# Four new tables for the order of work on the engines of a six-stage graph-network kernel

## The chip, the cores and the metric

The kernel runs on one core of a Trainium2 chip. The metric is the time on the device in microseconds (us), the median of several runs. Five engines work side by side: TensorE (PE in the profile, matmuls into PSUM banks), ScalarE (ACT), VectorE (DVE), GpSimd (POOL), and SyncE (SP), which here only issues DMAs. Each takes its own instructions strictly in the order in which they were written and stops at one that waits for a semaphore.

## The reference

128 graphs of 64 nodes with 256 features pass four graph layers; after each comes `x = layernorm(x + layer(x))`. Cut to what is computed, with `adj` the weighted adjacency matrix of a graph:

```python
def layer0(x):                       # hypergraph convolution, twice
    H = (adj != 0); B = 1 / H.sum(axis=1); Dn = 1 / (H @ adj[first row])
    conv = lambda x, W, b: Dn * (H @ (B * (H.T @ (x @ W.T)))) + b
    h = layernorm(relu(conv(x, W1, b1))) * gamma + beta
    return conv(h, W2, b2) + x
def layer1(x):
    q, k = split(x @ Wqk); v = x @ Wv
    w = mask * sum(q * (adj @ (k * mask)), -1) / 16
    return softmax(w, over nodes) * v
def layer2(x):                       # 8 heads of 32
    s = (q @ k.T) * 32 ** -0.5 * (adj + adj)
    return (softmax(s) @ v) @ Wo.T + bo
def layer3(x):
    xg = x * sigmoid(adj.sum(-1) * Wd + bd)
    QK = sigmoid(xg @ Wqk.T + bqk)
    s = (QK @ QK.T) / 16 * adj
    out = (s / (s.sum(-1) + 1e-6)) @ xg
    return relu(out @ Wl.T + bl + xg @ Wr.T)
```

## The kernel before

Four graphs (256 node rows, two tiles of 128) make a group; there are 32 groups. Every float32 product is made of two float16 parts: a value is cast to float16 on ScalarE (names ending in `h`), the remainder is formed on VectorE or GpSimd (names ending in `l`), and a product is three matmuls, L460 to L462. A block of 12 such matmuls with 256 columns is TensorE's common unit.

The work of a group is cut into six streams (0 to 5), each a Python generator on each engine that gives up control at every `yield`. In a step `s`, stream `k` works on group `s - k`, so six groups are under way at once and 32 groups take 37 steps. The first six and the last steps have fewer streams; a hardware loop over two steps holds the middle. Stream 0 is the first convolution of layer 0, stream 1 the second one and the first half of layer 1, stream 2 the softmax of layer 1 and the query of layer 2, stream 3 keys, values, scores and the exponentials, stream 4 the context, the output projection and the gate of layer 3, stream 5 the rest of layer 3.

What sets the order within a step is one list per engine, `ORDER_PE`, `ORDER_ACT`, `ORDER_DVE` and `ORDER_POOL`: each entry is the number of the stream that may do its next piece (the code up to its next `yield`). SyncE's order is written out apart and does not depend on the lists. All waits are on semaphores that are counted upwards, so any order that does not deadlock computes the same.

Pieces of TensorE that the text names: `m&d` (L519 to L525, HBh and wch into bank A), `pT` (L530, the turn of `Pf`), `z1`, `z01` and `z23` (the two halves of the projection with W1, together 24 matmuls), `rsum` (L556 to L560, sums of `rF` and of `rsq` over the features), `y0` (the product of `rF` and W2, in two halves `y0a` and `y0b`), `conv2` (y0 with P), `x1T` and `x2T` and `xgT` and `cxT` (L485, four transposes each), `u` and `ux`, `wT` (L595), `prT` (L598), `v1`, `q`, `k`, `v`, the two score blocks (L634), `eT0` and `eT1` (L645), the two context blocks (L658), `Wo`, `qk3`, `y3`, `s3`, `o2` (its L460 reads Wr), and the attention's row sums (L702).
On GpSimd: `gp` (L1217, bias of the gate), `xres` (L1217), `y0l`, `xl`, `rFl` (L1200), `Ssb0` and `Ssb1` (L1287, late<-late,Smx, the two shifts of the scores), the two sums of `rsq` (L1242, L1245), `xg` (L1299, late<-g,late), `am` (L1269), and for each layer norm K the small `veK`, `rsK`, `nbK`.
On VectorE: `preG` (L1176) and `rFl` of the second half (L999), both of two SBUF inputs; `o3` (L1171), the masked scores `Sm0`, `Sm1` (L1102), `rvar` (L1008), `wpr` (L1066), `Ql` (L1148), `HBl`, `x1Fl`, `x2Fl`, `ul`, `xgFl`, `PTl` and others of L894.
The tiles `late` hold several of these values.

SyncE copies the keys into a block-diagonal tile `Kbd` with four DMAs (L374) once their low half `kst` is there (L370), and the values likewise into `Vbd` (L384); between the two it issues the loads of the next step.

Of the kernel before, what the change touches and what calls it, by code (L numbers as in the profile page):

```python
# [40 lines left out]
QK3 = 0.25 / 16.0  # L41
HUGE = 3e38

ORDER_PE = [4, 2, 5, 4, 1, 3, 0, 5, 4, 3, 2, 0, 1, 5, 0, 2, 4, 0, 0, 5, 3, 1, 5, 3, 5, 2, 1, 3, 2, 1, 0, 3, 4, 0]
ORDER_ACT = [5, 0, 4, 2, 5, 1, 3, 5, 0, 4, 0, 3, 4, 0, 5, 4, 1, 0, 0, 0, 5, 2, 1, 0, 0, 0, 2, 3, 1, 4, 3, 2, 4, 3, 5]
ORDER_DVE = [0, 4, 0, 4, 0, 4, 0, 2, 0, 2, 4, 0, 1, 4, 2, 0, 0, 0, 2, 2, 5, 3, 5, 2, 4, 0, 1, 5, 1, 1, 0, 2, 2, 4, 2, 4, 4, 3, 3, 5, 3, 3, 1, 3, 5, 2, 5, 1, 0, 5, 5, 5, 3, 1, 1, 0, 4, 2, 0, 3, 0]
ORDER_POOL = [0, 0, 0, 1, 4, 1, 0, 3, 1, 1, 5, 1, 2, 2, 4, 2, 4, 0, 5, 3, 4, 0, 3, 0, 4, 1, 5, 5, 5, 0, 0, 0]

LAST_LAG = 5
STEPS = GROUPS + LAST_LAG  # L50
# [3 lines left out]
def build(nc, x, adj, adj_t, mask, mask_col, w1t, b1, gamma, beta, w2t, b2, wqk1t, wv1, wqt, bq, wkt, bk, wvt, bv,  # L54
          wot, bo, wqk3t, bqk, wlt, bl, wrt, wd, bd, out):
    ctx = ExitStack()
    with ctx:
# [213 lines left out]
        def run(eng, order, streams):  # L271


            def step(j, s, lo, hi):
                live = {k: streams[k](At(k, j, s)) for k in range(lo, hi + 1)}
                for k in order:
                    if k in live:
                        next(live[k], None)
                assert all(next(live[k], "end") == "end" for k in live)

            first = LAST_LAG + 1
            last = first + (GROUPS - first) // 2 * 2
            for s in range(first):
                step(None, s, 0, s)
            with eng.Fori(first // 2, last // 2) as j:
                for par in range(2):
                    step(j, par, 0, LAST_LAG)
            for s in range(last, STEPS):
                step(None, s, max(0, s - GROUPS + 1), LAST_LAG)
# [167 lines left out]
        def _(pe):  # L457
# [254 lines left out]

            run(pe, ORDER_PE, [stream0, stream1, stream2, stream3, stream4, stream5])


        @block.scalar
        def _(act):
# [168 lines left out]

            run(act, ORDER_ACT, [stream0, stream1, stream2, stream3, stream4, stream5])


        @block.vector  # L890
        def _(dve):
# [291 lines left out]

            run(dve, ORDER_DVE, [stream0, stream1, stream2, stream3, stream4, stream5])


        @block.gpsimd
        def _(pool):
# [123 lines left out]

            run(pool, ORDER_POOL, [stream0, stream1, stream2, stream3, stream4, stream5])

# [38 lines left out]
```

How the kernel before makes its waits and increments, by code:

```python
            def load_conv(at):  # L326
                if at.earlier(2):
                    sp.wait_ge(ev("x_lo"), at.n(-2)).then_inc(ev("sp_held"), 1)
                sp.dma_start(xin[:, at.par], at_group(xv, at)).then_inc(ev(f"x_in{at.par}"), 16)
                if at.earlier(2):
                    sp.wait_ge(ev("h_t"), at.n(-2)).then_inc(ev("sp_held"), 1)
                    sp.wait_ge(ev("w_lo"), at.chain(3, 3, -2)).then_inc(ev("sp_held"), 1)
                blocks(atA, adj_t, at, "at_in")
# [1 line left out]
            def load_residual(at):  # L335
                if at.earlier(2):
                    sp.wait_ge(ev("preB"), at.n(-2)).then_inc(ev("sp_held"), 1)
                sp.dma_start(xres[:, at.par], at_group(xv, at)).then_inc(ev(f"xres_in{at.par}"), 16)
# [1 line left out]
            def load_layer1(at):  # L340
                if at.earlier(2):
                    sp.wait_ge(ev("adj_masked"), at.n(-2)).then_inc(ev("sp_held"), 1)
                    sp.wait_ge(ev("w_masked"), at.n(-2)).then_inc(ev("sp_held"), 1)
                blocks(aC, adj, at, "C_in")
                sp.dma_start(mrow[:, at.par], mr[bass.ds(at.group(), 1)].rearrange("g o k -> (g o) k")
                             .broadcast_to([P, TOK])).then_inc(ev(f"C_in{at.par}"), 16)
                sp.dma_start(mcol[:, at.par], mask_col[bass.ds(at.group(), 1)].rearrange("g p t -> (g p) t")
                             ).then_inc(ev(f"C_in{at.par}"), 16)
# [107 lines left out]
        @block.tensor  # L456
# [31 lines left out]
            pe.wait_ge(ev("w2_scaled"), 1)
            for k in range(4):
```

## Time and profile before

| what | before |
|---|---|
| median of 3 runs | 1060.98 us (1060.03 to 1066.08) |
| profiled execution, span | 1059.4 us (nothing outside its span is recorded) |
| TensorE busy | 956.5 us, 90% |
| VectorE busy | 886.8 us, 84% |
| GpSimd busy | 777.8 us, 73% |
| ScalarE busy | 710.6 us, 67% |
| instructions | 32426 |

Busy time is a share of the span; fill and drain of the pipeline count in it. An idle engine is listed with what ended its idle time. The chain of waits is followed back from the last instruction; where it shows "issue", the engine waited for nothing that the profile records.

### The profile page before, as it was taken

To read this page: it belongs to the slowest core of one execution; us is meant where nothing else is said; L and a number is where in the kernel's file an instruction comes from. 1 tells how busy PE (TensorE), PEld (TensorE's weight loads), DVE (VectorE), ACT (ScalarE), POOL (GpSimd) and SP (SyncE) were. 2 spreads that over 40 slices of the span, in tenths; PEclk is the share of its full clock that TensorE was granted. 3 is DMA by queue.
4 is the path that set the end of the run, shared out by engine and by line. 5 is a ranking of instruction groups with operands and counts; after the bars stand their busy time and mean duration, and the time that the engine had idled before them with its cause. 6 is when DMAs were issued, how large, how long until landed. Compare 5 with 4: busy or idle time off the path is not lost.

```text
span 1059.4 us, 32426 instructions
## 1 busy us (share of the span) xinstructions
PE 956.5 (90%) x11164; PEld 808.6 (76%) x11164; DVE 886.8 (84%) x2564; ACT 710.6 (67%) x1516; POOL 777.8 (73%) x1163
## 2 busy tenths in 40 slices
PE   3368999999999999999999999999999999999873
PEld 2256788888888888888888888888888888887752
DVE  4346888898989989989998998989999998989862
ACT  2335677777776677777776677777776777776642
POOL 3155778778877788788877788788877887786542
PEclk9589999999999999999999999999999999999986
DMA  7110221222222122222222112222212112211110
GB/s 206 31 33 9 64 61 53 69 68 59 67 57 61 51 53 57 67 57 67 67 55 62 50 52 60 67 57 67 67 53 62 50 51 62 67 45 42 46 39 20
DMA packets 110231, 61.80 MB, mean 58 GB/s; under 512 B 57072, under 2 KB 105840, under 8 KB 110192
## 3 DMA queue, kind: packets, MB, share of 16 engines
q1 hardware_dynamic: 110192, 61.30, 22.2%
q8 instruction: 22, 0.36, 0.2%
q14 instruction: 17, 0.14, 0.0%
HBM read 35.83 MB, written 8.39 MB: 42 GB/s over the span
## 4 chain that ended last, share of the span: by engine, by line
DVE 33%; PE 25%; issue 14%; ACT 13%; POOL 12%; DMA 1%; DVEq 1%; SPq 0%; POOLq 0%; ACTq 0%
PE bank L460 7%; PE bank L462 6%; PE bank L461 6%; DVE preG L1176 4%; DVE rFl L999 3%; ACT x L735 3%; POOL y0l L1200 3%; ACT r L762 2%; DVE late L1171 2%; PE bank L485 2%; DVE ql L900 2%; PE bank L634 2%; DVE stG L947 2%; DVE PTl L894 2%; DVE xgFl L894 2%
## 5 line engine op out<-in xcount | busy, mean ns | idle before, releaser
L1102 DVE TENSOR_TENSOR late<-bank,acD 128x512 f32<-128x512 f32 x64 | 44.2, 690 | 51.3 <-PE bank L634 50.9
L735 ACT ACTIVATE x<-preB,nbB,rsB 128x256 f32<-128x256 f32 x64 | 35.0, 593 | 68.0 <-POOL nbB L1212 68.0
L460 PE MATMUL bank<-z1h,W 128*128 128x256 f16 x256 | 71.0, 277 | 3.1 <-DVE z1l L894 3.0
L461 PE MATMUL bank<-z1l,W 128*128 128x256 f16 x256 | 70.9, 277 | 0.0
L460 PE MATMUL bank<-W,rFh 128*128 128x256 f16 x256 | 70.8, 277 | 0.0
L462 PE MATMUL bank<-z1h,W 128*128 128x256 f16 x256 | 70.8, 277 | 0.0
L462 PE MATMUL bank<-W,rFl 128*128 128x256 f16 x256 | 70.5, 275 | 0.0
L461 PE MATMUL bank<-W,rFh 128*128 128x256 f16 x256 | 70.5, 275 | 0.0
L1287 POOL TENSOR_TENSOR late<-late,Smx 128x512 f32<-128x512 f32 x64 | 67.0, 1046 | 0.0
L735 ACT ACTIVATE late<-preG,nbG,rsG 128x256 f32<-128x256 f32 x64 | 34.9, 593 | 47.0 <-POOL nbG L1212 46.9
L1200 POOL TENSOR_TENSOR y0l<-y,y0h 128x512 f16<-128x512 f32 x32 | 55.5, 1736 | 1.5 <-ACT y0h L719 1.5
L1299 POOL TENSOR_TENSOR late<-g,late 128x512 f32<-128x512 f32 x32 | 53.5, 1672 | 2.9 <-ACT late L735 2.9
L762 ACT ACTIVATE r<-bank,b1c 128x256 f32<-128x256 f32 x128 | 49.8, 462 | 5.7 <-PE bank L462 5.7
L1248 POOL TENSOR_SCALAR rve<-rvar 128x2 f32<-128x2 f32 x32 | 7.2, 224 | 61.7 <-DVE rvar L1008 61.7
L1176 DVE SCALAR_TENSOR_TENSOR preG<-late 128x512 f32<-128x512 f32 x32 | 51.3, 1604 | 0.1
L1200 POOL TENSOR_TENSOR rFl<-r,rFh 128x512 f16<-128x512 f32 x32 | 37.2, 1163 | 19.1 <-ACT rFh L719 18.7
L1217 POOL TENSOR_TENSOR gp<-late,bdb 128x512 f32<-128x512 f32 x32 | 40.7, 1272 | 11.1 <-ACT late L842 11.1
L719 ACT ACTIVATE xgFh<-bank 128x512 f16<-128x512 f32 x32 | 19.1, 597 | 44.2 <-PE bank L485 44.2
L634 PE MATMUL bank<-Kbd,qh 128*64 128x256 f16 x512 | 47.1, 279 | 1.2 <-DVE vst L894 1.2
L485 PE MATMUL bank<-ident,x 128*128 128x128 f32 x256 | 42.2, 288 | 5.9 <-ACT x L735 2.7
L460 PE MATMUL bank<-xgFh,Wqk 128*128 128x256 f16 x128 | 36.2, 283 | 12.3 <-DVE xgFl L894 12.3
L645 PE MATMUL bank<-ident,E 128*128 128x128 f32 x256 | 40.3, 281 | 4.9 <-ACT E L831 4.9
(284 smaller groups left out, 4625.1 us busy)
## 6 DMA issues: line engine op xcount, KB each, us to landing
Vbd<-vst SPq DMA_DIRECT2D x128, 66.0 KB, 2.1
xin<-x SPq DMA_DIRECT2D x32, 256.0 KB, 2.7
xres<-x SPq DMA_DIRECT2D x32, 256.0 KB, 2.8
Kbd<-kst SPq DMA_DIRECT2D x128, 64.0 KB, 2.0
out<-late SPq DMA_DIRECT2D x32, 256.0 KB, 2.2
mrow<-mask SPq DMA_DIRECT2D x32, 128.0 KB, 3.1
atA<-adj_t SPq DMA_DIRECT2D x64, 32.0 KB, 2.3
aC<-adj SPq DMA_DIRECT2D x64, 32.0 KB, 2.1
```

Of the source, the lines that this page charges most:

```text
L460: pe.matmul(o, sh, mh, start=start, stop=False, skip_group_check=True)
L461: pe.matmul(o, sh, ml, start=False, stop=False, skip_group_check=True)
L462: return pe.matmul(o, sl, mh, start=False, stop=stop, skip_group_check=True)
L485: m = pe.transpose(o[:, c * TOK + t * P:c * TOK + (t + 1) * P], src[:, t, c * P:(c + 1) * P], ident_[:])
L634: m = pe.matmul(o[64 * b:64 * b + 64, c * 256:(c + 1) * 256], qq[:, c, tok], Kbd[:, :, hl, c, tok], start=(i == 0), stop=(i == 2), skip_gr ...
L735: m = act.activation(dst[:, t], pre[k][:, t], ACT.Identity, bias=nb[k][:, t:t + 1], scale=rs[k][:, t:t + 1])
L762: m = act.activation(r[:, 2 * i + c], (bA, bB)[i][:, c * TOK:(c + 1) * TOK], ACT.Relu, bias=b1c[:, 2 * i + c:2 * i + c + 1], scale=1.0 / WS)
L1102: dve.tensor_tensor(Sm[:, t], (bD0, bD1)[t][:].rearrange("p (h k) -> p h k", h=HEADS), acD[:, at.par, t:t + 1].broadcast_to([P, HEADS, NOD ...
L1176: dve.scalar_tensor_tensor(out=pre["G"][:].rearrange("p t k -> p (t k)"), in0=o3[:].rearrange("p t k -> p (t k)"), scalar=0.0, in1=x3[:, a ...
L1200: return pool.tensor_tensor(dst, a, b, ALU.subtract)
L1287: pool.tensor_tensor(Ssb[:, t], Sm[:, t], Smx[:, t:t + 1].rearrange("p t h -> p h t").broadcast_to([P, HEADS, NODES]), ALU.subtract).then_ ...
L1299: pool.tensor_tensor(xg[:], g2[:], x3[:, at.par], ALU.mult).then_inc(ev("xg"), 1)
```

## The change

Only the four lists change. Each keeps its length and how often each stream stands in it; every piece is still done once a step. What moves is where a piece stands among those of other streams.

```diff
-ORDER_POOL = [0, 0, 0, 1, 4, 1, 0, 3, 1, 1, 5, 1, 2, 2, 4, 2, 4, 0, 5, 3, 4, 0, 3, 0, 4, 1, 5, 5, 5, 0, 0, 0]
+ORDER_POOL = [0, 0, 0, 1, 1, 0, 4, 3, 5, 1, 1, 1, 1, 2, 2, 2, 4, 5, 4, 3, 0, 4, 3, 0, 0, 4, 5, 5, 5, 0, 0, 0]
...
```

GpSimd, in the loop, from the statistics of layer 2's norm to the product `xg`; first before, then with the change. `late<-late,blb` is the bias of `o2`.

```order
L1208 TENSOR_TENSOR rsF<-veF,powm 128x2
L1200 TENSOR_TENSOR rFl<-r,rFh 128x512
L1217 TENSOR_TENSOR late<-late,blb 128x512
L1287 TENSOR_TENSOR late<-late,Smx 128x512
L1212 TENSOR_SCALAR nbF<-mvF,rsF 128x1 x2
L1242 TENSOR_TENSOR rsq<-rsq 128x512
L1287 TENSOR_TENSOR late<-late,Smx 128x512
L1245 TENSOR_TENSOR rsq<-rsq 128x256
L1299 TENSOR_TENSOR late<-g,late 128x512
```

The same place with the change:

```order
L1217 TENSOR_TENSOR late<-late,blb 128x512
L1208 TENSOR_TENSOR rsF<-veF,powm 128x2
L1287 TENSOR_TENSOR late<-late,Smx 128x512
L1200 TENSOR_TENSOR rFl<-r,rFh 128x512
L1212 TENSOR_SCALAR nbF<-mvF,rsF 128x1 x2
L1287 TENSOR_TENSOR late<-late,Smx 128x512
L1242 TENSOR_TENSOR rsq<-rsq 128x512
L1245 TENSOR_TENSOR rsq<-rsq 128x256
L1299 TENSOR_TENSOR late<-g,late 128x512
```

`rFl` has moved behind the first shift of the scores, and both sums of `rsq` behind the second. Further up the list `gp` moved from ahead of `y0l` to behind `xl`, `SAl` ahead of `veB`, and `am` from behind `xg` to behind `nbB`.

VectorE, in the loop, from the second masked score to the statistics of layer 3's norm; first before.

```order
L1102 TENSOR_TENSOR late<-bank,acD 128x512
L894 SCALAR_TENSOR_TENSOR x1Fl<-bank,x1Fh 128x512
L1107 TENSOR_REDUCE Smx<-late 128x8
L1165 RECIPROCAL srec<-ssum 128x2
L894 SCALAR_TENSOR_TENSOR x2Fl<-bank,x2Fh 128x512
L1171 SCALAR_TENSOR_TENSOR late<-bank,srec,late 128x256 x2
L894 SCALAR_TENSOR_TENSOR ul<-bank,uh 128x512
L999 TENSOR_TENSOR rFl<-r,rFh 128x512
L1176 SCALAR_TENSOR_TENSOR preG<-late 128x512
L947 BN_STATS stG<-preG 128x6 x2
```

The same place with the change:

```order
L1102 TENSOR_TENSOR late<-bank,acD 128x512
L1165 RECIPROCAL srec<-ssum 128x2
L1107 TENSOR_REDUCE Smx<-late 128x8
L894 SCALAR_TENSOR_TENSOR x1Fl<-bank,x1Fh 128x512
L1171 SCALAR_TENSOR_TENSOR late<-bank,srec,late 128x256 x2
L894 SCALAR_TENSOR_TENSOR x2Fl<-bank,x2Fh 128x512
L1176 SCALAR_TENSOR_TENSOR preG<-late 128x512
L894 SCALAR_TENSOR_TENSOR ul<-bank,uh 128x512
L999 TENSOR_TENSOR rFl<-r,rFh 128x512
L947 BN_STATS stG<-preG 128x6 x2
```

`o3` now stands ahead of `x2Fl`, `x1Fl` behind the second maximum, and `preG` ahead of `ul` and `rFl`. Elsewhere on VectorE `xgFl` moved from ahead of `ql` to behind `rvar`, `HBl` from ahead of `y0` to behind it, `Ql` from behind `wpr` to ahead of the three small divisions (L982 to L988), the low half of `k` (L900, kst) from behind `Ql` to behind `preB`, and `z1l` behind `preC`.

On TensorE the order of a step was ctx0, wT, qk3, ctx1, y0b, k, m&d, y3, cxT, v, prT, pT, conv2, s3, z1, v1, Wo, z01, z23, o2, scores 0, x1T, row sums, scores 1, o1, x2T, u, eT0, q, ux, rsum, eT1, xgT, y0a. It is now wT, ctx0, y0b, ctx1, qk3, k, y3, m&d, cxT, v, pT, conv2, prT, s3, z1, v1, Wo, o2, z01, scores 0, z23, row sums, scores 1, x1T, o1, x2T, u, q, eT0, ux, eT1, rsum, y0a, xgT. On ScalarE the main moves are `x1Fh` to ahead of the first `rFh` (it stood behind it), and the second `relu` behind the norm of layer 1.

## Rows read from the trace of the kernel before

**Rows 1.** The page: the span.

```profile
span 1059.4 us, 32426 instructions
```

**Rows 2.** Windows: us, then busy time (instructions) of PE, PEld, DVE, ACT, POOL, clock, DMA.

```profile
200.00:400.00 200.00, 193.64 (x2344) 165.94 (x2342) 183.16 (x538) 143.91 (x311) 160.47 (x239) 1.00 0.22 59
```

**Rows 3.** Timeline, VectorE, `rvar`: start us, us, what [idle before <- releaser].

```profile
147.01 0.15 DVE L1008 SCALAR_TENSOR_TENSOR rvar<-bank,rmm 128x2 f32<-128x2 f32 x1
...
953.98 0.14 DVE L1008 SCALAR_TENSOR_TENSOR rvar<-bank,rmm 128x2 f32<-128x2 f32 x1
```

**Rows 4.** Chain of waits, one step: start us, us in the chain, what.

```profile
503.94 0.60 DVE xgFl L894
...
510.25 0.10 POOL gp L1217
...
511.47 1.82 POOL y0l L1200
...
513.33 0.28 PE bank L460
...
527.02 0.87 DVE late L1171 x2
```

**Rows 5.** Timeline, GpSimd, the tail of its list.

```profile
522.26 1.16 POOL L1200 TENSOR_TENSOR rFl<-r,rFh 128x512 f16<-128x512 f32 x1
...
525.64 0.49 POOL L1212 TENSOR_SCALAR nbF<-mvF,rsF 128x1 f32<-128x1 f32 x2
526.10 1.27 POOL L1242 TENSOR_TENSOR rsq<-rsq 128x512 f32<-128x512 f32 x1
527.33 1.03 POOL L1287 TENSOR_TENSOR late<-late,Smx 128x512 f32<-128x512 f32 x1
528.34 0.72 POOL L1245 TENSOR_TENSOR rsq<-rsq 128x256 f32<-128x256 f32 x1
529.02 1.72 POOL L1299 TENSOR_TENSOR late<-g,late 128x512 f32<-128x512 f32 x1
```

**Rows 6.** Timeline, VectorE, first masked score and two `preG`.

```profile
522.98 0.69 DVE L1102 TENSOR_TENSOR late<-bank,acD 128x512 f32<-128x512 f32 x1 [1.85 <-PE bank L634]
...
529.53 1.75 DVE L1176 SCALAR_TENSOR_TENSOR preG<-late 128x512 f32<-128x512 f32 x1
...
1033.38 0.69 DVE L1176 SCALAR_TENSOR_TENSOR preG<-late 128x512 f32<-128x512 f32 x1
```

**Rows 7.** Timeline, TensorE, one step.

```profile
500.07 0.16 PE L556 MATMUL bank<-ones,rFh 128*128 128x1 f16 x1 [0.36 <-DVE rFl L999]
...
500.92 0.63 PE L645 MATMUL bank<-ident,E 128*128 128x128 f32 x4
501.39 0.60 PE L485 MATMUL bank<-ident,late 128*128 128x128 f32 x4
...
504.60 0.28 PE L460 MATMUL bank<-xgFh,Wqk 128*128 128x256 f16 x1 [0.34 <-DVE xgFl L894]
...
512.84 0.44 PE L530 MATMUL bank<-ident,Pf 128*128 128x128 f32 x2
...
517.99 0.27 PE L460 MATMUL bank<-z1h,W 128*128 128x256 f16 x1
...
520.61 0.27 PE L460 MATMUL bank<-Wr,xgFh 128*128 128x256 f16 x1
...
522.79 0.66 PE L485 MATMUL bank<-ident,x 128*128 128x128 f32 x4
```

**Rows 8.** Waits: waiting piece and who ended it: us in total, times, longest.

```profile
PEld bank L658 <- DVE PTl L894: 10.0, 42, 0.4
```

**Rows 9.** Timeline, ScalarE, the cast of `r`.

```profile
521.55 0.63 ACT L719 ACTIVATE rFh<-r 128x512 f16<-128x512 f32 x1
```

**Rows 10.** Timeline, SyncE's queue, the copies into `Kbd`.

```profile
513.27 2.48 SPq L374 DMA_DIRECT2D Kbd<-kst  x4
```

**Rows 11.** The page: DMA issues, KB each, median us to landing.

```profile
Kbd<-kst SPq DMA_DIRECT2D x128, 64.0 KB, 2.0
```

More of the change, by code:

```diff
@@ L42 @@
 HUGE = 3e38
-ORDER_PE = [4, 2, 5, 4, 1, 3, 0, 5, 4, 3, 2, 0, 1, 5, 0, 2, 4, 0, 0, 5, 3, 1, 5, 3, 5, 2, 1, 3, 2, 1, 0, 3, 4, 0]
-ORDER_ACT = [5, 0, 4, 2, 5, 1, 3, 5, 0, 4, 0, 3, 4, 0, 5, 4, 1, 0, 0, 0, 5, 2, 1, 0, 0, 0, 2, 3, 1, 4, 3, 2, 4, 3, 5]
-ORDER_DVE = [0, 4, 0, 4, 0, 4, 0, 2, 0, 2, 4, 0, 1, 4, 2, 0, 0, 0, 2, 2, 5, 3, 5, 2, 4, 0, 1, 5, 1, 1, 0, 2, 2, 4, 2, 4, 4, 3, 3, 5, 3, 3, 1, 3, 5, 2, 5, 1, 0, 5, 5, 5, 3, 1, 1, 0, 4, 2, 0, 3, 0]
-ORDER_POOL = [0, 0, 0, 1, 4, 1, 0, 3, 1, 1, 5, 1, 2, 2, 4, 2, 4, 0, 5, 3, 4, 0, 3, 0, 4, 1, 5, 5, 5, 0, 0, 0]
+ORDER_PE = [2, 4, 1, 4, 5, 3, 5, 0, 4, 3, 0, 1, 2, 5, 0, 2, 4, 5, 0, 3, 0, 5, 3, 1, 5, 2, 1, 2, 3, 1, 3, 0, 0, 4]
+ORDER_ACT = [0, 5, 2, 5, 1, 4, 5, 0, 3, 0, 4, 3, 4, 0, 5, 5, 1, 4, 0, 2, 0, 1, 0, 0, 2, 0, 0, 1, 3, 4, 3, 3, 2, 4, 5]
+ORDER_DVE = [4, 0, 4, 0, 2, 4, 0, 2, 0, 4, 0, 1, 0, 4, 5, 0, 2, 0, 2, 0, 2, 5, 0, 1, 2, 3, 4, 5, 1, 1, 2, 0, 2, 4, 2, 4, 3, 4, 3, 5, 3, 3, 5, 3, 1, 5, 2, 5, 1, 0, 5, 5, 1, 3, 0, 1, 3, 0, 2, 0, 4]
+ORDER_POOL = [0, 0, 0, 1, 1, 0, 4, 3, 5, 1, 1, 1, 1, 2, 2, 2, 4, 5, 4, 3, 0, 4, 3, 0, 0, 4, 5, 5, 5, 0, 0, 0]
 LAST_LAG = 5
```

## The prediction

> **What bounds the kernel now.** I read the busy line first, then the windows, the period, the chain of waits, and last the timelines of the engines where the chain passes. The span is 1059.4 us [rows 1]. The median of the shown runs is 1060.98, so 1.6 us lie around the profiled span; every sum below is a difference and is set on the median. In the filled pipeline TensorE is busy 193.64 of 200 us at full granted clock, VectorE 183.16, GpSimd 160.47 [rows 2]. So TensorE alone leaves some 3% to win, and only in the filled stretch. The reader should see that this stretch repeats: `rvar` starts at 147.01 and at 953.98 [rows 3], 27 intervals of 29.89 us. The other 252 us fill and drain the pipeline.
>
> The chain of waits shows why a step takes 29.89 us and not TensorE's 29. It runs through VectorE up to `rvar`, then down the GpSimd list (`gp` and `y0l` among it), enters TensorE at the second convolution at 513.33, stays there for twelve microseconds, and goes back to VectorE through `x2Fl`, `o3` (the tile `late` of L1171) and `rFl` [rows 4]. `xgFl`, `gp` and `o3` stand in it only because they are listed there; nothing in the chain reads their results.
>
> **What leaves the chain.** (1) `gp` moves behind `y0l` and `xl`. That frees 1.22 us, from 510.25 to 511.47 (the chain gives 0.10 to `gp` itself and the rest to no one, but GpSimd does nothing else in it) [rows 4]. `y0l` still needs `y0h`, which ScalarE can give no earlier than some 0.6 us after `y0`, so I count 1.0. (2) `xgFl` moves behind `rvar`: 0.60. (3) `o3` moves ahead of `x2Fl`, into a place where VectorE would otherwise stand by: up to 0.82. VectorE now idles 1.85 us before the first masked score [rows 6], and in the new TensorE list the first score comes one 1.31 us block earlier, so that idle shrinks. Counting these alone the step would be 29.89 - 1.0 - 0.6 - 0.8 = 27.5, below what TensorE can do. So this chain stops being the bound, and the question is which takes over.
>
> **TensorE's own work.** From the first row-sum matmul to the end of the first score block it takes 500.07 to 522.79, 22.72 us. Of this 0.34 is the wait for `xgFl` and 0.27 the wait for `y0l` (two transposes and the wait take 512.84 to 513.33, 0.49, where four take 0.47) [rows 7], and 10.0 us in 42 waits are for `PTl` [rows 8], some 0.3 a step. The new list puts `xgT` after `y0`, and both context blocks and `y0` ahead of `qk3`, so these three are covered: `xgFl` has 2.6 us of matmuls to hide in. Waits left out elsewhere (before `rsum` 0.36, before `x2T` 0.15 as an estimate) give about 28.1 to 28.4 for a step with no wait. That is the floor.
>
> **What takes over: the tail of the GpSimd list.** `rsum` on TensorE needs both sums of `rsq`. Before, `rFl` (its first half) stood ahead of the score shifts, and the longer sum ahead of the second shift. Now both are listed after: `Ssb0`, `rFl`, `nbF`, `Ssb1`, `rsq`, `rsq`. And on TensorE the turn of `x1` moves behind the second score block, on ScalarE `x1Fh` ahead of the first `rFh`. So `rFl` cannot start before all that. With 0 at the start of the second half of `z` (the block that now follows the first scores):
> - TensorE: 1.31 (half of the 2.62 from 517.99 to 520.61), row sums of the attention 0.15 (estimate: 4 matmuls of a kind of which 18 take 0.85), second scores 0.8 (520.61 to 522.79 holds one block of 1.31 and the first scores), `x1T` and its landing 0.6 [rows 7]: 2.86.
> - ScalarE: `x1Fh` 0.5, `rFh` 0.63 [rows 9]: 3.99.
> - GpSimd: `rFl` 1.16, `nbF` 0.46, `Ssb1` 1.01, `rsq` 1.23 and 0.68 [rows 5]: 8.53.
> - The lock between VectorE and GpSimd. Alone, `preG` takes 0.69; beside `xg` it takes 1.75, and `xg` takes 1.72 where the equally large `rsq` takes 1.27 [rows 5, 6]. Two instructions with two SBUF inputs do not run together: each delays GpSimd by about 0.45. Before, only `rFl` and `preG` met `xg`, after the last `rsq`. Now `preG` comes directly behind `x2Fl`, two instructions ahead of `rFl`, and by the sum both meet `Ssb1` and `rsq`, ahead of `rsum`: 0.9. That is 9.43.
> - To TensorE's start 0.36, as before `rsum` now [rows 7]: 9.79.
> - TensorE from `rsum` to the end of the first scores: 22.72 less `eT1` 0.47 (now ahead of `rsum`), less `z23` 1.31, less the covered waits 0.34 + 0.27 + 0.3 = 20.0.
>
> The sum is 29.8, with estimated terms that I rounded upwards by some 0.1; I take 29.7, 0.19 below 29.89. This is 27 x 0.19 = 5 us. With one lock instead of two it would be 27 x 0.6 = 16. In short, gains of 2.4 us in the old chain are nearly all taken by a new one.
>
> The Trainium skill (SBUF — State Buffer, section on two separate sides) says that VectorE and GpSimd share one port pair as an exclusive lock, held for a whole instruction, for VectorE operations with two SBUF inputs. The 0.69 against 1.75 agrees. By that rule `HBl`, too, which moves from ahead of `y0` to behind it, would stand behind `xres`; no row here shows `HBl` beside a long GpSimd instruction.
>
> **Smaller edits.** `am` moves from the tail to behind `nbB`, where GpSimd waits for VectorE's statistics; its cover is that wait, and if it is gone it delays `nbC` by at most 1.27 (what the larger `rsq` takes [rows 5]), some microseconds ahead of its use. `m&d` moves behind `y3`: the three small divisions on VectorE now wait for it, and `Pf` and `pT` stand behind them with only `cxT` and `v` (1.9 us) as cover, against about 2.1 of need. Between nothing and 1.2 us (if VectorE is late); I take 0 since `pT` is at TensorE's place with 0.2 to spare and keep the upper end for the range. `z1l` moves behind `preC`, with some 0.9 us to spare. Fill and drain keep their dependences; ten steps with some 0.4 us either way, 0 within 4.
>
> **Rivals.**
> (A) **TensorE alone sets the step.** If `preG` slips in ahead of `Ssb1`, or ScalarE's `rFh` comes sooner than I have it, the sums are ready when TensorE is. Against it: the sum of the GpSimd tail has no slack to lose. For it: 8.53 without locks gives 28.9, near TensorE's floor. Step 28.7: 1061 - 27 x 1.19 = 1029; range 1020 to 1045.
> (B) **The gain does not come at all:** `m&d` behind `y3` makes `pT` late by 0.3, on top of the forecast. Step 30.0: 1064; 1059 to 1070.
> (C) **Slower: the scores wait for `Kbd`.** The low half of `k` moves on VectorE behind `y3l`, `Pl`, `preB` and `pcol` (some 1.6 us), and the first scores come 1.31 us earlier. SyncE issues the four copies at 513.27 and needs 2.48 for them, the last lands 2.0 after its issue [rows 10, 11]: about 4.2 from the end of `kst` to data. Before, the scores began 4.8 us later than that. Now 4.8 - 1.6 - 1.3 = 1.9 are left, less 0.6 because TensorE is quicker between, less 0.7 because the small divisions wait. If the lock holds VectorE 1 us or more ahead of `kst` (`Ql` behind `y0l`, `wpr` behind `xl`), it decides: about 0.9 us a step more, 27 x 0.9 = 24, 1085; from 1072 to 1095. By the Trainium skill (SBUF — State Buffer, same section) `HBl` is one more that waits ahead of `kst`, which would make C likelier.
>
> **How the numbers follow.** A measurement of this kernel tells about 1% from no change; that is 1050.4 to 1071.6. Forecast 0.42: step 29.7, 1061 - 5 = 1056, its own range 1046 to 1061 with 0.08 of its chance below 1050. A 0.26, B 0.13, C 0.15, and 0.04 for something not seen, half to each side. Faster: 0.08 + 0.26 + 0.02 = 0.36. Within: 0.34 + 0.13 = 0.47. Slower: 0.15 + 0.02 = 0.17. The range reaches to the middle of A and leaves out most of C: 1026 to 1074.
>
> **What would show it.** `rvar` every 29.7 us. `y0l` starts some microseconds before the second convolution and no longer releases it. TensorE's wait before `rsum` is the longest of its waits, and is ended by GpSimd's `rsq` (L1245), not by `rFl`. `preG` and `rFl` stay above 1.1 us, `Ssb1` or `rsq` above 1.4. A is right if TensorE has no wait over 0.2 before `rsum` and the step is below 29. B shows as a wait before L530 for `Pf`, C as one before the first L634 for the DMA into `Kbd`. The forecast is wrong in its mechanism if `rsq` ends long before `rsum` starts.

## The result, and the profile after

The change takes **1075.89 us** (median of 4 runs, 1071.0 to 1077.48) against 1062.18 (4 runs) for the kernel before: ratio 1.0124, 95% interval 1.0091 to 1.0157. It is slower by 13.7 us by the medians (13.2 by the ratio), where I had forecast 1056 and a range that ended at 1074. The sign and the range both missed.

The page of the changed kernel (span, then busy time) has the same 32426 instructions as before, and every engine is busy for as long or less:

```profile
span 1073.0 us, 32426 instructions
...
PE 949.5 (88%) x11164; PEld 806.2 (75%) x11164; DVE 860.9 (80%) x2564; ACT 708.5 (66%) x1516; POOL 761.7 (71%) x1163
```

Since no engine is busy for longer, the 13.6 us between the spans (1073.0 against [rows 1]) are waiting. To place them I date the steps by `rvar`, one per step, as in [rows 3]. The timeline of the changed kernel at the 6th, 7th and 32nd:

```profile
187.08 0.15 DVE L1008 SCALAR_TENSOR_TENSOR rvar<-bank,rmm 128x2 f32<-128x2 f32 x1
...
218.46 0.15 DVE L1008 SCALAR_TENSOR_TENSOR rvar<-bank,rmm 128x2 f32<-128x2 f32 x1
...
963.99 0.15 DVE L1008 SCALAR_TENSOR_TENSOR rvar<-bank,rmm 128x2 f32<-128x2 f32 x1
```

and the kernel before at the 6th and 7th:

```profile
176.96 0.15 DVE L1008 SCALAR_TENSOR_TENSOR rvar<-bank,rmm 128x2 f32<-128x2 f32 x1
...
206.84 0.15 DVE L1008 SCALAR_TENSOR_TENSOR rvar<-bank,rmm 128x2 f32<-128x2 f32 x1
```

The filling steps end with the sixth `rvar`: it is at 187.08 instead of 176.96, 10.1 us late; the seventh is 11.6 late. The last is 10.0 late (963.99 against [rows 3]). So in between, the loop gives a little back: from the ninth `rvar` on, a step takes 29.82 us against 29.87. What I predicted, the loop, did almost what I said. What I had set to nothing, the fill, lost nearly everything. In 200 us of the loop, columns as in [rows 2], TensorE is busy for 2 us less than before and VectorE for 9 us less:

```profile
200.00:400.00 200.00, 191.66 (x2332) 164.57 (x2330) 174.49 (x529) 145.66 (x313) 159.17 (x246) 1.00 0.23 62
```

**One step of the loop.** Timelines of GpSimd, VectorE and TensorE, to be held against [rows 5 to 7]:

```profile
508.23 1.16 POOL L1200 TENSOR_TENSOR rFl<-r,rFh 128x512 f16<-128x512 f32 x1
...
509.94 1.48 POOL L1287 TENSOR_TENSOR late<-late,Smx 128x512 f32<-128x512 f32 x1
511.38 1.75 POOL L1242 TENSOR_TENSOR rsq<-rsq 128x512 f32<-128x512 f32 x1
513.22 0.73 POOL L1245 TENSOR_TENSOR rsq<-rsq 128x256 f32<-128x256 f32 x1
```

```profile
509.80 0.72 DVE L1176 SCALAR_TENSOR_TENSOR preG<-late 128x512 f32<-128x512 f32 x1
...
511.33 0.68 DVE L999 TENSOR_TENSOR rFl<-r,rFh 128x512 f16<-128x512 f32 x1
```

```profile
514.00 0.18 PE L556 MATMUL bank<-ones,rFh 128*128 128x1 f16 x1 [0.59 <-POOL rsq L1245]
```

GpSimd works its tail with hardly a pause, and the row sums on TensorE start when `rsq` is done. `z23` starts at 504.07, `rsum` at 514.00: 9.93 us. The waits of the whole kernel (who waited <- for whom: us, times, longest) confirm which wait has replaced `rFl`'s, and name a second one, in the first five steps only. Of its 17.3 us, 9.5 are the very first wait, which the kernel before has too; in the second to fifth step `m&d` waits 1.49, 3.01, 2.38 and 0.86 for `HBl`, together 7.7 us, where the kernel before waits 0.17:

```profile
PE bank L556 <- POOL rsq L1245: 22.4, 30, 5.4
...
PE bank L519 <- DVE HBl L894: 17.3, 5, 9.5
```

**One step of the fill.** In the third filling step the two `HBl` on VectorE take 2.12 us, in the fourth 2.54, both times beside `xres` and then `y0l` on GpSimd (the GpSimd rows are of the third step), and in the fifth 0.98, beside `xres` alone; in the loop, and in the kernel before, the pair takes 0.6. These holds are 3.8 us of the 7.7. The rest is the new place itself: `HBl` stands behind `y0`, 0.87 us of VectorE, and `y0` waits for TensorE. In the second step `HBl` is not held at all (0.60), but the `y0` ahead of it waits 3.09 us for TensorE. The last row is TensorE's `m&d`, which waits 3.01 us for it:

```profile
78.33 2.12 DVE L894 SCALAR_TENSOR_TENSOR HBl<-HT,be,HBh 128x128 f16<-128x128 f16 x2
...
104.89 2.54 DVE L894 SCALAR_TENSOR_TENSOR HBl<-HT,be,HBh 128x128 f16<-128x128 f16 x2
```

```profile
77.86 1.27 POOL L1217 TENSOR_TENSOR xres<-xres,b2b 128x512 f32<-128x512 f32 x1
79.16 1.15 POOL L1200 TENSOR_TENSOR y0l<-y,y0h 128x512 f16<-128x512 f32 x1
```

```profile
80.51 0.29 PE L519 MATMUL bank<-HBh,HT 128*128 128x128 f16 x1 [3.01 <-DVE HBl L894]
```

### The profile page after: what moved, and what is told of

It reads as the page before. It is cut to its first block, busy times and chain, and to the rows that moved or that the text cites. A ratio compares the mean times of both kernels' runs of the same rounds, so it can differ in the third digit from the quotient of the medians.

```text
span 1073.0 us, 32426 instructions
## 1 busy us (share of the span) xinstructions
PE 949.5 (88%) x11164; PEld 806.2 (75%) x11164; DVE 860.9 (80%) x2564; ACT 708.5 (66%) x1516; POOL 761.7 (71%) x1163
## 4 chain that ended last, share of the span: by engine, by line
PE 40%; POOL 19%; DVE 19%; issue 15%; ACT 4%; DMA 1%; SPq 1%; POOLq 1%; DVEq 0%; ACTq 0%
PE bank L460 10%; PE bank L462 9%; PE bank L461 9%; POOL late L1287 6%; POOL rsq L1242 5%; PE bank L658 3%; PE bank L485 3%; DVE preC L1075 2%; POOL rsq L1245 2%; POOL rsC L1208 2%; DVE stC L947 2%; DVE kst L900 2%; DVE stB L947 2%; DVE cFl L894 2%; PE bank L560 1%
## 5 line engine op out<-in xcount | busy, mean ns | idle before, releaser
L1200 POOL TENSOR_TENSOR y0l<-y,y0h 128x512 f16<-128x512 f32 x32 | 42.7, 1333 | 64.1 <-ACT y0h L719 64.1
L1287 POOL TENSOR_TENSOR late<-late,Smx 128x512 f32<-128x512 f32 x64 | 78.7, 1229 | 1.6 <-DVE Smx L1107 1.6
L719 ACT ACTIVATE late<-bank 128x512 f32<-128x512 f32 x32 | 19.1, 597 | 78.4 <-PE bank L462 78.4
L864 ACT ACTIVATE qt<-bank,bqkc 128x256 f32<-128x256 f32 x64 | 26.9, 470 | 60.6 <-PE bank L462 60.6
L1200 POOL TENSOR_TENSOR SAl<-SA,SAh 128x256 f16<-128x256 f32 x32 | 21.5, 671 | 59.2 <-ACT SAh L719 59.2
L762 ACT ACTIVATE r<-bank,b1c 128x256 f32<-128x256 f32 x128 | 52.6, 461 | 7.8 <-PE bank L462 7.8
L1242 POOL TENSOR_TENSOR rsq<-rsq 128x512 f32<-128x512 f32 x32 | 53.7, 1678 | 1.7 <-ACT rsq L770 1.7
L460 PE MATMUL bank<-x1Fh,Gm 128*128 128x256 f16 x128 | 35.2, 275 | 16.4 <-DVE x1Fl L894 16.4
L462 PE MATMUL bank<-Wv,x2Fl 128*128 128x128 f16 x256 | 45.7, 222 | 0.0
L461 PE MATMUL bank<-Wv,x2Fh 128*128 128x128 f16 x256 | 45.7, 222 | 0.0
```

The lines of the kernel that those rows point to most:

```text
L460: pe.matmul(o, sh, mh, start=start, stop=False, skip_group_check=True)
L461: pe.matmul(o, sh, ml, start=False, stop=False, skip_group_check=True)
L462: return pe.matmul(o, sl, mh, start=False, stop=stop, skip_group_check=True)
L762: m = act.activation(r[:, 2 * i + c], (bA, bB)[i][:, c * TOK:(c + 1) * TOK], ACT.Relu, bias=b1c[:, 2 * i + c:2 * i + c + 1], scale=1.0 / WS)
L1200: return pool.tensor_tensor(dst, a, b, ALU.subtract)
L1242: pool.tensor_tensor(rsq[:, 0:2], rsq[:, 0:2], rsq[:, 2:4], ALU.add).then_inc(ev("sq_sum"), 1)
```

## The experiments

The lists are given below by pieces, in the names of the text ahead (`PTl0` and `PTl1` are the first and second `PTl`, `relu0` and `relu1` the two halves of `r`, L762, `nC` the norm ahead of `x1F`). "Sixth" is the time of the sixth `rvar`, "step" the mean from the ninth to the last, both from the one profiled execution; that of the new drain (1067.73 us) and of the fill on TensorE and ScalarE (1084.15) was the slowest of its kernel. Each ratio is to runs of the kernel before on the same chip, whose medians are 1061.86 to 1064.26 us.

| kernel | median us (runs) | ratio to before, 95% | sixth | step |
|---|---|---|---|---|
| before | see the ratios | 1 | 176.96 | 29.871 |
| the change | 1075.89 (4) | 1.0124 (1.0091 to 1.0157) | 187.08 | 29.821 |
| new loop | 1064.69 (9) | 1.0021 (1.0011 to 1.0032) | 176.37 | 29.817 |
| new fill | 1076.2 (4) | 1.0124 (1.0083 to 1.0165) | 186.36 | 29.846 |
| new drain | 1062.4 (12) | 1.0003 (0.9993 to 1.0013) | 177.19 | 29.872 |
| `HBl` | 1068.41 (4) | 1.0068 (1.0046 to 1.0089) | 179.53 | 29.816 |
| `relu` | 1065.6 (1) | no interval | 183.49 | 29.686 |
| `kst` | 1092.67 (4) | 1.0274 (1.0251 to 1.0297) | 184.64 | 30.522 |
| old lists, `HBl` late | 1154.79 (4) | 1.0857 (1.0831 to 1.0884) | 189.99 | 33.047 |
| `rsq` first | 1078.82 (1) | no interval | 193.59 | 29.842 |
| three edits | 1098.21 (1) | no interval | 185.68 | 30.880 |
| same, old ends, `PTl` late | 1100.33 (5) | 1.0359 (1.0334 to 1.0384) | 178.56 | 31.182 |
| same, old ends | 1093.11 (5) | 1.0287 (1.0268 to 1.0305) | 177.96 | 30.867 |
| idle matmuls | 1075.15 (1) | no interval | 187.24 | 29.824 |
| new fill, `HBl` early | 1069.31 (8) | 1.0050 (1.0031 to 1.0068) | 179.93 | 29.849 |
| its TensorE and ScalarE | 1080.67 (5) | 1.0153 (1.0131 to 1.0175) | 197.11 | 29.874 |
| its VectorE and GpSimd | 1071.78 (6) | 1.0072 (1.0051 to 1.0092) | 186.75 | 29.872 |
| best loop, old ends | 1059.0 (7) | 0.9954 (0.9937 to 0.9971) | 177.34 | 29.687 |

### Fill, loop and drain apart

```diff
-            def step(j, s, lo, hi):
+            def step(j, s, lo, hi, order):
...
-                step(None, s, 0, s)
+                step(None, s, 0, s, order[0])
...
-                    step(j, par, 0, LAST_LAG)
+                    step(j, par, 0, LAST_LAG, order[1])
...
-                step(None, s, max(0, s - GROUPS + 1), LAST_LAG)
+                step(None, s, max(0, s - GROUPS + 1), LAST_LAG, order[2])
```

Each engine has three lists now, and one of the three is new, the others old. New loop alone:

> The new lists in the hardware loop only (26 steps), the old ones in the six steps that fill the pipeline and the five that drain it. Theory F (the loss lies in fill and drain, where the streams that are missing leave other pieces on the path): rvar of the sixth group at 176.96 +- 0.5 us as before, 26 steps of 29.82 instead of 29.87, drain as before: 1062.2 - 1.3 = 1061. Rival R (the loss comes from where the engines stand when the loop of the new lists is entered, some 1.5 us at its first step and more to settle): 1065 to 1074, with steps above 30 in the first part of the loop.

New fill alone:

> The new lists in the six fill steps only. Theory F: rvar of the sixth group 10 us later than before (187.08 against 176.96), loop and drain as before: 1062.2 + 10 = 1072. Rival R: the fill alone costs little, 1062 to 1065.

New drain alone:

> The new lists in the five drain steps only. Theory F: from the last rvar to the end 109.0 us instead of 105.4, so 1062.2 + 3.6 = 1066. Rival: the drain is a chain of single groups in either order, 1062; the 3.6 us come from the state in which the new loop leaves it.

Measured: +2.8, +14.3 and +0.5 us. Theory F was right for the fill, whose loss came out 4 us larger than expected; it was 4 us too low for the loop, and wrong for the drain, where its rival came true. The fill alone has the whole loss, with the same ratio as the change; the drain costs nothing that can be told. The new loop gains 3.6 us up to the last `rvar` (950.36 against [rows 3]), 1.3 of it in its first step alone, and gives them back, and more, on the way into the old drain (110.8 us from there to the end against 105.4). The parts add up to some 4 us more than the whole: where two lists meet, a step is longer or shorter than either's own (28.6 us from old to new, 33.3 and 32.4 from new to old).

### `HBl` ahead of `y0` again

```diff
 VectorE:
-... HBh y0 HBl cx1 Ql Dbg ...
+... HBh HBl y0 cx1 Ql Dbg ...
```

> The new lists everywhere, with one swap undone in the list of VectorE: HBl (the low part of H times 1/B) stands ahead of y0 again. Theory H (in the fill m&d on TensorE waits for HBl, which waits behind y0 and then for the port beside GpSimd's xres, 2.05 us in the third step): the intervals of rvar 24.33, 26.96, 28.18 of the fill fall by 1.8, 2.5 and 1 to 2.5 us, the loop stays at 29.8: 1075.9 - 6 = 1070. Rival Z (the fill is lost to z1l behind preC and to the second relu behind the norm of layer 1): 1074 to 1076.

The sixth `rvar` comes at 179.53, 7.6 us earlier, and the median falls by 7.5. One instruction pair that changes places with another is about half of the loss: 7.5 us of 13.7 by the medians, 5.9 of 13.2 by the ratios. The loop does not notice it (29.816). The other way round, the old lists everywhere with the pair behind `y0`:

```diff
 VectorE, list of before:
-... wrm rinv1 HBl y0 cx1 ...
+... wrm rinv1 y0 HBl cx1 ...
```

> The kernel before with one thing of the change alone: HBl behind y0 on VectorE. Theory: the fill intervals grow as those of the change did through it, by 1.8, 2.7 and some 2.5 us (22.57, 22.19, 22.82 before), and the loop stays within 0.3 of 29.87 or grows a little, since y0 is earlier and HBl has slack there: 1062 + 7 = 1069. Rival: HBl only costs together with the other moves: 1062 to 1064.

It takes 1154.79, 92 us more than before, many times what I expected: 13 us of it up to the sixth `rvar`, and then 3.2 a step in the loop. The tile's line in the kernel before and in this one (ns of one, lowest, median, highest, then first and last start):

```profile
L894 DVE SCALAR_TENSOR_TENSOR HBl<-HT,be,HBh x64: 287/332/352, 33.0 to 926.6; 128x128 f16<-128x128 f16 x64
```

```profile
L894 DVE SCALAR_TENSOR_TENSOR HBl<-HT,be,HBh x64: 344/1273/1373, 32.7 to 1018.1; 128x128 f16<-128x128 f16 x64
```

and one of its steps, on VectorE and GpSimd, with the wait that follows on TensorE over the whole kernel:

```profile
521.84 2.54 DVE L894 SCALAR_TENSOR_TENSOR HBl<-HT,be,HBh 128x128 f16<-128x128 f16 x2
```

```profile
521.70 1.26 POOL L1217 TENSOR_TENSOR xres<-xres,b2b 128x512 f32<-128x512 f32 x1
522.92 1.31 POOL L1217 TENSOR_TENSOR gp<-late,bdb 128x512 f32<-128x512 f32 x1
```

```profile
PE bank L519 <- DVE HBl L894: 73.4, 32, 9.5
```

The first `HBl` stands until `xres` is done, the second until `gp` is done: 2.54 us instead of 0.6. In the old GpSimd list two long instructions follow `wcl`, in the new one only `xres`, and `y0l`, which must wait for `y0h` in the loop and so leaves a gap. Besides, the old TensorE list has `m&d` directly behind `k`, so nothing covers the 2.5 us. Of the 73.4 us of waiting 9.5 are the first wait, which the kernel before has too; the other 63.9, over 31 steps, are most of the 92. In the change's own loop `HBl` is not held, since there `HBh` ahead of it is: 1.08 us instead of 0.40, beside `xres`.

### What the rest of the fill is

The new chain of waits in the third filling step (start, us in the chain, what), and the same place of the kernel before:

```profile
87.96 0.88 DVE preC L1075 x2
88.84 0.59 DVE z1l L894
89.43 0.67 DVE stC L947 x2
...
91.93 0.51 POOL nbC L1212 x2
...
92.46 1.09 ACT x L735 x2
93.55 0.72 ACT r L762 x2
```

```profile
86.40 1.45 ACT r L762 x4
87.85 0.52 ACT rFh L719
88.36 0.97 ACT x L735 x2
```

Before, ScalarE does all of `relu` and the first `rFh` and then the norm C. Now half of `relu` stands behind norm C, and norm C behind `z1l`, the statistics of VectorE and three small instructions of GpSimd. I took this for the second half of the loss.

```diff
 ScalarE, with HBl ahead of y0:
-... relu0 nC relu1 x1Fh rFh0 ...
+... relu0 relu1 rFh0 nC x1Fh ...
```

> The new lists with HBl ahead of y0 (as in the run before) and, on ScalarE, the second relu and the first rFh ahead of the norm of layer 1 again. Theory: in the third step the path runs preC, stC, mvC, nbC, the norm, and only then the relu, rFh and the squares; with the relu first, the interval of rvar there falls from 24.20 to some 22.5, the next from 24.58 to about 24 (the scores' wait for Kbd stays), the loop stays at 29.82. Rival: z1l behind preC holds it just as long, 24.2 stays.

The fill did not get faster: the sixth `rvar` is at 183.49, 4.0 us later than without the edit, and the third step takes 27.05 us instead of 24.20. But this cannot be laid on the edit, since TensorE's mean clock in that step was 0.80 here and 0.93 there (what that is worth follows below), and the kernel of all three edits, which has this one too, takes 23.95 for it at 0.93. What the edit brought is in the loop, 29.686 us a step. Next I looked at the fourth filling step, whose chain passes through the DMAs into `Kbd`:

```diff
 VectorE, on top of the last:
-... wpr y3l Pl preB pcol kl ...
+... wpr kl y3l Pl preB pcol ...
```

> As the kernel before it, and on VectorE the low half of k ahead of y3l, Pl and preB. Theory: the wait of the first scores for Kbd in the fourth step goes (2 us), the interval of rvar there falls from 24.58 to below 23; with all three the fill is as fast as before (sixth rvar at 177 +- 1) and the whole takes 1062 to 1065 against 1068.4 with HBl alone. Rival: the fill is bound by the new order on TensorE (scores ahead of z23, x1T later), and the fourth interval stays above 24: 1066 to 1068.

Missed, and by much. `kl` (the low half of `kst`) needs the high half from ScalarE, and moved forward it stops VectorE in every step. Over the whole kernel it waits for ScalarE's `kst` (L818) 36.8 us, in 31 steps, where it did not wait before.

Then the clock. In stretches of 7 us in the fill the granted clock changes between about 0.5 and 1.0, that is between TensorE's levels of 1.2 and 2.4 GHz:

```diff
+            def warm(at, n):
+                if at.j is None and 1 <= at.fixed <= 3:
+                    for _ in range(n):
+                        pe.matmul(bG[:, 0:D], W1[:, 0, 0, 0:P], W1[:, 0, 0, 0:D], start=True, stop=True,
+                                  skip_group_check=True)
...
+                warm(at, 6)
...
+                warm(at, 5)
...
+                warm(at, 12)
```

> The change with idle matmuls added on TensorE in the second to fourth step alone: six of 256 rows ahead of pT, five ahead of z01, twelve ahead of rsum, into a bank that is rewritten afterwards. Of the 10 us that the filling steps lost, the steps hold waits that were covered before (the lock at HBl, the third statistics ahead of the other work of VectorE) and stretches of half clock. Theory K: 4 to 6 us are the clock, which falls because TensorE stands idle; with the idle matmuls the granted clock from 59 to 87 us rises above 0.8 and the sixth rvar starts at 184 or earlier (187.1 in the change). Rival: the clock follows from other things, or costs nothing since TensorE waits anyway; the sixth rvar then starts at 187 to 190, later by what the idle matmuls take.

The windows of the change, then of this kernel (columns as in [rows 2]):

```profile
59.00:66.00 7.00, 5.41 (x34) 3.90 (x34) 2.72 (x7) 2.15 (x5) 2.62 (x6) 0.55 0.38 94
66.00:73.00 7.00, 3.88 (x36) 3.00 (x34) 1.86 (x3) 5.28 (x11) 3.03 (x3) 0.96 0.00 0
73.00:80.00 7.00, 4.16 (x53) 3.48 (x50) 5.76 (x21) 0.94 (x2) 3.94 (x9) 1.00 0.13 31
80.00:87.00 7.00, 5.13 (x35) 4.01 (x36) 3.44 (x14) 1.61 (x4) 1.73 (x4) 0.51 0.00 0
```

```profile
59.00:66.00 7.00, 4.40 (x45) 3.58 (x42) 2.36 (x7) 4.13 (x10) 2.14 (x5) 1.00 0.32 94
66.00:73.00 7.00, 5.30 (x31) 3.85 (x32) 2.03 (x7) 2.69 (x6) 3.15 (x3) 0.53 0.01 2
73.00:80.00 7.00, 4.46 (x52) 3.80 (x50) 4.72 (x16) 0.94 (x2) 3.85 (x8) 0.99 0.12 28
80.00:87.00 7.00, 6.47 (x41) 4.74 (x42) 3.40 (x14) 1.61 (x4) 1.74 (x4) 0.51 0.00 0
```

The mean clock of these 28 us is 0.755 in the one and 0.757 in the other, the low stretches only lie elsewhere, and the sixth `rvar` is at 187.24 instead of 187.08. The idle matmuls did not raise the clock, so this run cannot price it.

The other profiles can, in part. In the kernel before the same 28 us have a mean clock of 0.88, with `HBl` early 0.90. And the old lists in the fill were profiled six times. The third step of the kernel before, then the same step of `same, old ends`, whose fill has the same lists:

```profile
75.10:97.29 22.19, 17.50 (x163) 13.68 (x161) 13.18 (x46) 11.06 (x24) 12.15 (x21) 0.92 0.04 11
```

```profile
73.13:98.33 25.20, 20.75 (x165) 15.91 (x163) 14.38 (x47) 11.05 (x24) 12.17 (x21) 0.79 0.04 9
```

The same work takes 3.0 us longer at the lower clock (the other four profiles give 22.2 at 0.92 three times, and 25.2 at 0.79 once). By the sixth `rvar` the six lie within 2.2 us; in two of them it is the second step that is the longer one, 25.3 us at 0.69 against 22.6 at 0.79 in the kernel before. So such a shift is worth some 3 us a step, and theory K has the right order of size.

Over the whole kernel the clock does not make most of the loss. The kernel before takes 1059.9 to 1063.5 us in its 16 executions with a mean clock of 0.969 or more, and 1063.1 to 1066.6 in the 13 at 0.965 or 0.966. The change takes 1071.0 in its one execution at 0.973, some 10 more than the kernel before at such a clock, and 1074.8 to 1077.5 in the three at 0.967 and 0.968, some 13 more. With `HBl` early 1.5 to 3.8 us less are needed at 0.972 to 0.974, and 5 to 8 less at 0.969. In all three pairs of profiles that differ by `HBl` alone the late place has the lower clock between 59 and 87 us (0.76 against 0.90 in the change, 0.76 against 0.89 with the fill alone new, 0.62 against 0.88 in the old lists). But the old lists alone vary between 0.76 and 0.89 there, so theory K is neither shown nor excluded for a part of the loss.

Last, the fill was split by engines, with `HBl` early and everything outside the fill old. First all four new lists:

> The new lists in the six filling steps alone, with HBl ahead of y0 in them; the old lists in loop and drain. With the new lists in the fill alone the kernel took 1076 us, 14 more than before. Theory: HBl is worth the 7.5 us in the fill that it was worth in the whole change, and the rest stays: 1067 to 1070. Rival: most of the rest belonged to the new loop and its passage into the old drain; then 1062 to 1065.

New lists on TensorE and ScalarE only:

> The fill with the new lists on TensorE and ScalarE, and the old ones on VectorE and GpSimd (HBl thus ahead of y0); loop and drain old. If the rest of the loss lies in the order on TensorE and ScalarE (the third norm ahead of relu, the score blocks ahead of the row sums), this has all of it, 1067 to 1070. If it lies on VectorE (z1l behind preC, kst behind Pl and preB) or GpSimd, this is within 1.5 us of before, 1061 to 1063.

New lists on VectorE and GpSimd only:

> The other half: the fill with the new lists on VectorE (HBl ahead of y0) and GpSimd, the old ones on TensorE and ScalarE; loop and drain old. If the rest of the loss lies on VectorE or GpSimd, 1067 to 1070; if on TensorE or ScalarE, 1061 to 1063. Both halves above 1065 would mean that it is spread, or that it comes from how the lists fit each other.

All four: +5.1 us, of which 3.0 up to the sixth `rvar` and 2.5 more in the first step of the old loop. The first theory holds. The halves cost +16.4 and +7.5 us. The first is far worse than the whole; the second's interval touches the whole's, but its sixth `rvar`, at 186.75, is 6.8 us later. Both halves were profiled at a mean clock of 0.76 between 59 and 87 us, the whole at 0.89, so a part of their excess may be the clock's. Both above 1065 was the case named for a loss that is spread or comes from how the lists fit each other: neither old half takes the rest of the loss away, and the first adds much of its own.

### Is there a better loop?

By the forecast `rsq` sets the step; so both sums go ahead of the second score shift.

```diff
 GpSimd:
-... nbF Ssb1 sqs1 sqs2 xg ...
+... nbF sqs1 sqs2 Ssb1 xg ...
 TensorE:
-... ux eT1 rsum y0a xgT
+... ux rsum y0a eT1 xgT
```

> The new lists with the tail of GpSimd's list turned: both sums of rsq ahead of the second shift of the scores, and on TensorE the second turn of E behind rsum and y0a. Theory P (a loop step is set by the path x1T, x1Fh, rFh, rFl, nbF, Ssb1, rsq, rsq, rsum and on through TensorE): rsum starts 1.2 us earlier after z23, its wait for rsq falls from 0.6 to below 0.3, the step falls from 29.82 to 29.0 to 29.3. Rival Q (another path has the same length, through the statistics of layers 1 and 2 to veF and o2's bias on GpSimd): 29.6 to 29.8. The fill is as slow as with the change.

`rsum` did come 1.15 us earlier (8.78 behind `z23` instead of 9.93), and the step stayed at 29.84. The fill, expected to be as slow as the change's, is slower: the sixth `rvar` is at 193.59, 6.5 later. An edit that the loop covers costs again where there are few streams, here at a mean clock of 0.70 between 59 and 87 us against 0.76, which may be a part of it. The waits of the whole kernel show what took over in the loop (9.5 of the 24.8 is again the first wait):

```profile
DVE PTl L894 <- ACT PTh L719: 53.7, 60, 1.7
...
PE bank L519 <- DVE HBl L894: 24.8, 20, 9.5
```

The work from `rsum` through `eT1`, `PTh`, `PTl`, `ql`, `rvar` and `HBl` to `m&d` is about as long as the path that was shortened. With all three edits together:

> The new lists with three edits in every step: HBl back ahead of y0, relu and the first rFh ahead of the third norm on ScalarE, and both rsq sums ahead of Ssb1 (eT1 behind rsum on TensorE). The last of these alone made rsum 1.3 us earlier and left the step at 29.84, since TensorE then waited for HBl through eT1, PTh, PTl, rvar and y0. Theory: those are the two long paths of a step, and with both shortened it falls to 29.2 to 29.3 us. Rival: the path over eT1 and PTl sets the step also without the lock at HBl; then it stays at 29.6 to 29.8.

The same with the old lists in fill and drain (the run that this text calls the one before it is the one that follows here):

> As the run before it, with both PTl left where the new lists have them. Theory: the waits of VectorE for PTh lie off the critical path, and it is within 3 us of that run, 1046 to 1052. Rival: they lie in it, through rvar, xgFl and y0; then it is slower than that run by 27 x 0.3 = 8 us.

And, with those old ends, `PTl0` behind `wpad` and `PTl1` behind `rvar`:

> The old lists in fill and drain, and in the loop those of the three edits together, with the first PTl moved behind wpad and the second behind rvar on VectorE, so that VectorE does not stand waiting for ScalarE's PTh. Theory: a step of about 29.2 us, 27 x 0.65 less than before, some 1046 to 1050 in all. Rival: the later PTl makes the context block late on TensorE, and the step is 29.6 or more, 1056 to 1062.

All three missed by more than a microsecond a step: 30.88, 30.87 and 31.18. The chain of the first of them, from `rsum` to `Pf`:

```profile
520.42 0.18 PE bank L556
...
523.22 0.61 ACT PTh L719
...
523.86 0.69 DVE PTl L894
...
525.38 0.15 DVE rvar L1008
...
528.05 1.32 DVE HBh L971
...
529.66 0.35 DVE HBl L894
...
532.64 0.62 ACT Pf L748 x2
```

From `rsum` on, TensorE's turn of the scores now comes second, and everything that the next step begins with hangs behind it, on VectorE's one list: `PTl`, `ql`, `rvar`, then `HBh` (1.32, beside `xres`), `HBl`, `y`. There the path over `eT1` bounds the step, and `HBl` ahead of `y0`, harmless in the change's loop, lies in it. How much of the extra microsecond is that and how much the norm behind `relu` was not split. The `relu` kernel has both of these edits and takes 29.69, and the turned tail alone costs the change's loop 0.02; only together do they cost 1.2. Taking `PTl` out of the way made it worse by 0.3 a step, and the context blocks on TensorE (L658) wait for it there, 4.8 us in 9 waits between 400 and 700 us: VectorE's stand was not the price, `PTl` itself is in the path.

What was left was the better loop of the `relu` kernel, with old lists at both ends:

> The old lists in fill and drain, in the loop the new ones with HBl ahead of y0 and relu and the first rFh ahead of the third norm on ScalarE. In a single look that loop took 29.69 us a step against 29.87 before. Theory: 27 x 0.18 = 5 us less in the loop and 2 to 3 us given back on the way into the old drain, as with the new loop alone: 1059 to 1061. Rival: the gain of the step was that one execution's; then 1062 to 1065.

It takes 1059.0 us against 1064.26 of the kernel before on the same chip: **0.9954, 0.9937 to 0.9971, faster than both kernels**. The step is 29.687, as in the one run of the `relu` kernel, and the total is what I expected. Its last `rvar` is 6.5 us earlier than in [rows 3]:

```profile
947.48 0.15 DVE L1008 SCALAR_TENSOR_TENSOR rvar<-bank,rmm 128x2 f32<-128x2 f32 x1
```

Its seven executions have a mean clock of 0.967 or 0.968 and take 1058.6 to 1059.8; on the same chip the kernel before takes 1062.6 to 1063.8 in its four at that clock, so the gain is not the clock's. The largest wait on TensorE in 200 us of its loop, 400 to 600:

```profile
PE bank L460 <- DVE x1Fl L894: 3.4, 7, 0.5
```

In this stretch GpSimd's `rsq` ends no wait of TensorE any more. With `relu1` and `rFh0` ahead of the norm, `rFl` and the sums come earlier (`rsum` 9.80 behind `z23` instead of 9.93), and most of each step's chain is TensorE's own matmuls. That is rival A's direction, at a sixth of its size (0.18 of 1.19 us a step).

## Why the prediction was wrong

- **The step that failed: "Fill and drain keep their dependences; ten steps with some 0.4 us either way, 0 within 4".** It measured 10.1 us at the sixth `rvar`, 11.6 at the seventh, and the new fill alone has the whole difference (1.0124). The dependences are indeed the same. But in the fill an engine has few streams to fill its waits with, and a move that a full step covers is not covered there. This is shown for `HBl` and, in one profile that also has a lower clock, for the turned tail (0.02 us a step in the loop, 6.5 us in the fill); for the rest of the loss it is argued. I argued from covers ("what hides it") for every edit in the loop and did not ask which of these covers exist when only two or three streams are live. The drain was rightly nothing.
- **`HBl`.** The prediction has it: by the Trainium skill (SBUF — State Buffer, section on two separate sides) `HBl` behind `y0` would stand behind `xres`, and by that rule the trace after agrees: 2.12 us in the third step beside `xres` (1.27) and `y0l` (1.15). I used the rule only for the loop and rival C. In the loop it costs nothing, in the fill it is worth 7.5 us by the medians when undone in the change (5.9 by the ratios; with the fill alone new, 1.0124 against 1.0050, which is 7.9). Of this the lock is about half: 3.8 of the 7.7 us that `m&d` waits; the other half is that `HBl` stands behind a `y0` that has to wait. With 7.5 in the sum the forecast would have been 1064.
- **The loop's step, 29.7.** Measured 29.82; the terms added up to 29.8 and I rounded them down. The GpSimd path was right in kind and size: 9.93 us from `z23` to `rsum` (9.79 forecast), TensorE's part 19.9 (20.0). Within the 9.93 there is some luck: GpSimd's last sum ends at 9.88 (9.43 forecast), and TensorE starts 0.05 behind it (0.36 forecast). That it is not the only bound, the prediction did not see: with `rsum` 1.15 us earlier the step stays at 29.84. TensorE's wait before `rsum` is its largest, ended by `rsq` (L1245), 0.59 us, and not by `rFl`.
- **The lock, two times 0.45.** `Ssb1` takes 1.48 where `Ssb0` takes 1.04, `rsq` 1.75 where it took 1.27 [rows 5]: 0.44 and 0.48. But my sign for it, `preG` and `rFl` above 1.1 us, was wrong: they take 0.72 and 0.68. They start first and are not held; in the kernel before they started second, and took 1.75 [rows 6] and 1.16. GpSimd then paid once, behind the last sum (`xg` 1.72 [rows 5], now 1.28), and pays twice now, ahead of `rsum`. VectorE no longer pays; its busy time falls from 886.8 to 860.9 us.
- **`y0l`** starts 2.15 us after GpSimd is free and has left the path, as said.
- **Rival B** (`pT` late) and **rival C** did not come in the loop; the wait for `Kbd` is seen once in the fill (0.65 us) and three times behind the last `rvar` (0.83, 0.54 and 0.66). **Rival A** is not what the change did, although `preG` does start ahead of `Ssb1` (509.80 against 509.94), its first condition: the sums are late all the same; the last kernel above goes some way towards it.
- The forecast's gain of 5 us was to come from 27 steps at 0.19; it was 0.05 a step, 1.3 us. The 13.6 us between the two spans are +11.6 in fill and first loop step, -1.6 in the rest of the loop, and +3.6 between the last `rvar` and the end (109.0 against 105.4), where the five profiles with the old lists in loop and drain and `HBl` early in both have between 105.4 and 109.3 us; so the last term cannot be laid on the lists.

**Still open:** some 5 us of the fill beside `HBl`. Moving `relu` ahead of the norm did not bring them back (one execution, at a lower clock), nor did old lists on either pair of engines. How much of the whole loss is the lower clock in the fill, and whether the new order causes it, is open too.

## What to carry to other kernels

Cost a new order separately for each stage with its own set of live streams: before you write "covered by", name the piece that covers it in the emptiest step. Where one set of lists serves fill, loop and drain, give each its own; here the same tables held a small gain in the loop and a large loss in the fill, and lists of their own for the loop, with three pieces moved in them, turned 1.2% slower into 0.5% faster. And change such lists as a set: new ones on two engines beside old ones on the others were worse, clearly so in one case of two, than all four new.

## What the hardware showed that I had not expected

- Of two instructions that hold each other off, the one that starts second is held: `preG` takes 0.72 us when it starts ahead of `Ssb1`, and 1.75 behind `xg` [rows 6]; `rFl` takes 0.68 ahead of `rsq`.
- An instruction with one tensor from SBUF is held as well. `HBh` (float16 in and out, with a scalar per partition) takes, in the loop of the change, beside an `xres` of 1.27 us that starts at 519.47:

```profile
519.87 1.08 DVE L971 TENSOR_SCALAR HBh<-HT,be 128x128 f16<-128x128 f16 x2
```

  The pair takes 0.40 in the third step of the kernel before. Here it ends 0.2 us after `xres` does.
- A pair of short instructions can be held twice: `HBl`, 0.6 us of work, took 2.54 beside two GpSimd instructions that follow without a gap.
- In the fill the granted clock goes between about 0.5 and 1.0 from one 7 us stretch to the next, and 23 more matmuls a step in three steps moved the low stretches but left the mean (0.76). With the same lists a filling step took 22.2 us at a mean clock of 0.92 and 25.2 at 0.79.
